# Order of the attention products within a step of a fused feed-forward and attention stage

## The reference

```python
x = x + 0.5 * ffn(layernorm(x))
x = x + attn(layernorm(x))
x = x + 0.5 * ffn(layernorm(x))

def attn(z):                                  # windows of 64 rows, 16 heads of 16
    q, k, v = split(z @ w_qkv)
    q, k = rmsnorm(q) * ln_w, rmsnorm(k) * ln_w
    att = softmax(causal(q @ k.T / 4))
    return (att @ v) @ w_proj

def ffn(z):                                   # 8 experts, 2 a row, capacity 640, and a shared part
    shared = (silu(z @ sg) * (z @ su)) @ sd   # 2048 hidden columns
    return shared + routed(z, router, rg, ru, rd)   # 1024 hidden columns an expert
```

## Time and profile before

| | us |
|---|---|
| median of 3 runs | 2125.52 (2121.11 to 2128.36) |
| profiled execution | 2136.3 |
| its span in the trace | 2134.6 |
| TensorE matmul busy | 2091.1 (98%) |
| VectorE busy | 1356.4 (64%) |
| ScalarE busy | 963.4 (45%) |
| GpSimd busy | 491.3 (23%) |

### The profile page before, as it was taken

How to read it: one execution, slowest core, us unless ns; L and a number is a source line. 1 busy time by engine, 2 the same in 40 slices (tenths; PEclk the granted TensorE clock), 3 DMA queues, 4 the chain that set the end, 5 groups by cost and what they waited for, 6 DMA issues and landing times.

```text
span 2134.6 us, 37638 instructions
## 1 busy us (share of the span) xinstructions
PE 2091.1 (98%) x13844; PEld 1910.7 (90%) x13844; DVE 1356.4 (64%) x3108; ACT 963.4 (45%) x1910; POOL 491.3 (23%) x433
## 2 busy tenths in 40 slices
PE   8999999999999999999998999999999999999999
PEld 7888899999998788888887887888999999988888
DVE  7666556666665688887888876666466666633333
ACT  3333235555553566556665542333455555522222
POOL 2423211121212232233334433222112211200000
PEclk9999999999999999999999999999999999999999
DMA  9231225554446344443544432231245444441010
GB/s 272 96 120 58 75 63 131 133 144 108 104 94 186 93 105 109 114 119 91 121 111 124 114 107 78 71 98 39 78 104 114 102 96 110 118 124 60 30 60 20
DMA packets 295976, 218.70 MB, mean 102 GB/s; under 512 B 69241, under 2 KB 276525, under 8 KB 295792
## 3 DMA queue, kind: packets, MB, share of 16 engines
q1 hardware_dynamic: 278128, 194.92, 32.5%
q0 software_dynamic: 17664, 21.38, 5.8%
HBM read 129.48 MB, written 93.23 MB: 104 GB/s over the span
## 4 chain that ended last, share of the span: by engine, by line
PE 86%; DVE 7%; issue 3%; POOL 2%; DMA 1%; SPq 1%; ACT 0%; another core or an unknown queue 0%; DVEq 0%; POOLq 0%; ACTq 0%
PE gate_up_p L347 28%; PE quad L347 25%; PE out_p L385 22%; PE misc L385 4%; PE quad L555 2%; PE quad L570 1%; PE misc L539 1%; PE misc L411 1%; PE quad L571 1%; DVE qk L1154 1%; DVE p_s L1169 1%; DVE h_s L1034 1%; PE misc L422 1%; POOL w L1406 1%; PE misc L403 1%
## 5 line engine op out<-in xcount | busy, mean ns | idle before, releaser
L347 PE MATMUL gate_up_p<-zh,w 128*128 128x512 f32 (+2 forms) x2368 | 705.5, 360 | 3.2 <-DVE h_s L1034 2.4
L721 ACT CAST hh<-h_s 128x512 fp32r<-128x512 f32 (+2 forms) x511 | 276.1, 540 | 699.6 <-DVE h_s L1034 631.3
L347 PE MATMUL quad<-zh,w 128*128 128x512 f32 (+2 forms) x1728 | 481.9, 346 | 0.0
L347 PEld LDWEIGHTS gate_up_p<-zh,w 128*128 128x128 f32 x2368 | 431.2, 189 | 53.8 <-DVE h_s L1034 3.7
L385 PE MATMUL out_p<-w,hh 128*128 128x256 f32 x2808 | 458.3, 282 | 5.9 <-DVE hl L1050 3.1
L385 PEld LDWEIGHTS out_p<-w,hh 128*128 128x128 f32 x2808 | 402.9, 189 | 29.3 <-DVE hl L1050 5.7
L347 PE MATMUL gate_up_p<-zl,w 128*128 128x512 f32 (+2 forms) x1184 | 422.8, 357 | 0.0
L1050 DVE TENSOR_TENSOR hl<-h_s,hh 128x512 fp32r<-128x512 f32 (+2 forms) x431 | 247.2, 573 | 136.5 <-ACT hh L721 120.3
L1034 DVE TENSOR_TENSOR h_s<-gate_up_p,sg_s 128x512 f32<-128x512 f32 (+2 forms) x296 | 178.5, 603 | 241.4 <-PE gate_up_p L347 223.6
L347 PEld LDWEIGHTS quad<-zh,w 128*128 128x128 f32 x1728 | 308.6, 188 | 24.8
L347 PE MATMUL quad<-zl,w 128*128 128x512 f32 (+2 forms) x864 | 295.5, 342 | 0.0
(11 more groups left out here) (189 smaller groups left out, 2530.5 us busy)
## 6 DMA issues: line engine op xcount, KB each, us to landing
stage<-in_L_ffn_rg SPq DMA_DIRECT2D x128, 128.0 KB
stage<-in_L_ffn_ru SPq DMA_DIRECT2D x128, 128.0 KB
stage<-in_L_ffn_rd SPq DMA_DIRECT2D x128, 128.0 KB
heads_d<-qkh SPq DMA_DIRECT2D x128, 128.0 KB
q_t<-heads_d SPq DMA_DIRECT2D x32, 384.0 KB, 4.6
k_t<-heads_d SPq DMA_DIRECT2D x64, 192.0 KB, 4.8
slots_d<-empty SPq DMA_DIRECT2D x16, 662.5 KB, 7.6
zh_d<-zh SPq DMA_DIRECT2D x16, 512.0 KB
```

The source lines that it names most:

```text
L347: last = pe.matmul(dst, a, b, start=(k == 0), stop=(k == 3 * n - 1))
L721: nc.scalar.copy(hh[:, n % 2, 0:ncol], h_s[:, n % 2, 0:ncol]).then_inc(sm["hh_done"], 1)
```

## The change

Three engines' orders within a step change; the instructions stay the same.

- TensorE: the probability transposes come ahead of y's, the q and k product ahead of the projection; the v product comes after up(n); the value products come last in the step, after down(n) and the z transposes. The new waits: q and k wait for `a_ysum`, v for `a_vl` of the tile before. New order: gate(n), [early down], probability transposes, y transposes, q and k product, projection, up(n), v product, [late down], gate(n+1), head transposes, scores, up(n+1), preparation, down(n), z transposes, value products.
- ScalarE: silu(n) ahead of `yh`.
- VectorE: both parts of the preparation (`others`) come early, ahead of `yl`; `pl` ahead of the addition to x; `normal` after `values_low`; the row sums and their reciprocal after the heads' low part, just ahead of masking; `azl` ahead of `outputs`.

```diff
-            def qkv(t, out):
+            def qk_products(t, out):
                 if out is None:
                     pe.wait_ge(sm["a_zl"], t + 1)
                     wait(pe, sm["a_masked"], t - 1)
+                else:
+                    pe.wait_ge(sm["a_ysum"], out + 1)
+                split_product(quad[:, 0, :], [(azh[:, k, :], azl[:, k, :], aw[:, 0, k, 0:2 * C], aw[:, 1, k, 0:2 * C])
+                                              for k in range(KC)], KC).then_inc(sm["a_qk"], 1)
+
+            def v_product(t, out):
+                wait(pe, sm["a_vl"], t)
+                if out is not None:
+                    pe.wait_ge(sm["a_o"], out + 1)
+                split_product(quad[:, 1, 0:C], [(azh[:, k, :], azl[:, k, :], aw[:, 0, k, 2 * C:3 * C], aw[:, 1, k, 2 * C:3 * C])
+                                                for k in range(KC)], KC).then_inc(sm["a_v"], 1)
...
                 gate(n, b % 2, c, buf, SB)
-                if out is not None:
-                    y_transpose(out)
                 if early_down:
                     down_of(*chunk_before(f, phase, b, c))
                 if probs is not None:
                     prob_transposes(probs, z, uses)
                 if out is not None:
+                    y_transpose(out)
+                if z is not None:
+                    qk_products(z, out)
+                if out is not None:
                     project(out)
+                up(n, b % 2, c, buf, SB)
                 if z is not None:
-                    qkv(z, out)
-                up(n, b % 2, c, buf, SB)
+                    v_product(z, out)
...
-                if probs is not None:
-                    values(probs, z, keys, out)
                 if c == 0:
                     out_free(f, phase, b)
                 down_of(f, phase, b, c)
...
                     z_transpose(ahead, uses_by(pf, pb, c + 1))
+                if probs is not None:
+                    values(probs, z, keys, out)
...
+                silu(n, SB)
                 if out is not None:
                     act.wait_ge(sm["a_yt"], out + 1)
                     wait(act, sm["a_x"], out)
                     nc.scalar.copy(yh[:, :, :], chunks(quad[:, 1, 0:C])).then_inc(sm["a_yh"], 1)
-                silu(n, SB)
...
-                if ahead is not None and c:
-                    normal(ahead)
+                if s:
+                    others(s - 1, 0)
+                    others(s - 1, 1)
+                if ahead is not None and not c:
+                    stats(ahead)
+                if out is not None:
+                    dve.wait_ge(sm["a_yh"], out + 1)
+                    v.tensor_tensor(yl[:, :, :], chunks(quad[:, 1, 0:C]), yh[:, :, :], ALU.subtract).then_inc(sm["a_yl"], 1)
+                if probs is not None:
+                    dve.wait_ge(sm["a_ph"], probs + 1)
+                    v.tensor_tensor(pl[:, :, :], pairs, ph[:, :, :], ALU.subtract).then_inc(sm["a_pl"], 1)
                 if out is not None:
                     dve.wait_ge(sm["a_x"], out + 1)
                     v.tensor_tensor(xtile(out), quad[:, 1, C:2 * C], xtile(out), ALU.add).then_inc(sm["a_o"], 1)
...
-                if z is None or c:
-                    h_product(n, SB)
-                if z is not None and c:
+                h_product(n, SB)
+                if z is not None:
                     qk_normal(z)
+                if z is not None:
                     values_low(z)
...
+                if ahead is not None:
+                    normal(ahead)
                 if c:
                     fused_low(n)
                 if z is not None:
                     heads_low(z)
+                if probs is not None:
+                    row_sums(probs)
+                    inverse_sums(probs)
                 if keys is not None:
                     masked(keys)
...
                 banks(s)
-                if probs is not None:
-                    outputs(probs)
                 if ahead is not None:
                     dve.wait_ge(sm["a_zh"], ahead + 1)
                     v.tensor_tensor(azl[:, :, :], chunks(misc[:, 1, 0:C]), azh[:, :, :], ALU.subtract).then_inc(sm["a_zl"], 1)
+                if probs is not None:
+                    outputs(probs)
                 fused_low(n + 1)
```

More of the change, by code:

```diff
@@ L546, in scores @@
                     pe.wait_ge(sm["a_vl"], z + 1)
-                elif out is not None:
+                if out is not None and z is None:
                     pe.wait_ge(sm["a_o"], out + 1)
@@ L1212, in fused_step @@
                 n = chunk(f, phase, b, c)
-                if out is not None:
-                    dve.wait_ge(sm["a_yh"], out + 1)
-                    v.tensor_tensor(yl[:, :, :], chunks(quad[:, 1, 0:C]), yh[:, :, :], ALU.subtract).then_inc(sm["a_yl"], 1)
                 if ahead is not None and c:
@@ L1231, in fused_step @@
                     v.tensor_tensor(xtile(out), quad[:, 1, C:2 * C], xtile(out), ALU.add).then_inc(sm["a_o"], 1)
[L1232 to L1235, removed]
-                if probs is not None:
-                    row_sums(probs)
-                    inverse_sums(probs)
-                    dve.wait_ge(sm["a_ph"], probs + 1)
-                    v.tensor_tensor(pl[:, :, :], pairs, ph[:, :, :], ALU.subtract).then_inc(sm["a_pl"], 1)
-                if ahead is not None and not c:
-                    normal(ahead)
                 if z is not None:
@@ L1246, in fused_step @@
                     v.tensor_scalar(qke[:, :], ssq[:, :], 1.0 / C, RMS_EPS, ALU.mult, ALU.add).then_inc(sm["a_qke"], 1)
-                if z is None or c:
-                    h_product(n, SB)
-                if z is not None and c:
+                h_product(n, SB)
+                if z is not None:
                     qk_normal(z)
+                if z is not None:
                     values_low(z)
-                elif z is not None:
-                    values_low(z, (0,))
-                    qk_normal(z)
-                    values_low(z, (1,))
-                    h_product(n, SB)
-                others(s - 1, 1)
+                if ahead is not None:
+                    normal(ahead)
                 if c:
```

## The result

| | before | after |
|---|---|---|
| median, us (same chip) | 2126.6 | 2192.7 (2188.8 to 2193.8) |
| ratio to before, 95% interval | | 1.0317 [1.0301, 1.0333] |
| span of the profiled execution | 2134.6 | 2187.1 |
| the profiled execution itself | 2136.3 | 2188.8 |

The change costs 66 us. The forecast was 2168, and the time lies above its range (2131 to 2186). Its sign and its mechanism hold. Two terms of its sum don't: the one for the clock, which was nothing, and the one for the preparation, which was +4.

A forecast was written before the change was run, and what follows sets the result against it. TensorE was taken to bound regular work in the fused stage. Regular blocks +37, preparation +4 and tail +3 made +44 us on the profiled execution; against the median 2125.5, less a little, 2168 us, range 2131 to 2186.

The forecast's parts named there:

- p to M: Regular step, from projection start (p) to masking start (M): M = p + 8.2 us, with row sums and reciprocal now before masking.
- M to the exponential, M to y: After masking start: exponential ends M + 5.6 us, `half_s` runs M + 5.63 to 6.9, multiply by 1/sum due M + 5.8.
- The blocked end: VectorE held by GpSimd's `half_s`: multiply ends M + 7.2, low part M + 8.35, against 6.2 and 6.85 us without blocking.
- c = 0 pairs: Steps c=6 to c=0 to c=2: 37.5 us with blocking, 35.4 without, 34.0 before; TensorE waits of 2.8, 0.7 and 0.6 us.
- Clock: Falls to the 1.2 GHz level after TensorE waits: some 1.7 us each, none in the sum, up to five in the range.
- Preparation: Next feed-forward's preparation, from step 26: some 20 us exposed ahead of `yl`, less waits that go; +4, between -8 and +10.
- A: The forecast case: blocking and late value products, 2168 us, 2150 to 2186 by preparation's bounds and clock falls; chance 0.58.
- Silu's table load on y's path: ScalarE, silu ahead of `yh`: table load 1.28 us on y's path, binding only without blocking, projection then at M + 8.3.
- Rival D: Silu's table load costs more than its 1.28 us; an end wait at each switch would give 2208 us; chance 0.03.
- B: The multiply by 1/sum gets ahead of `half_s` (margin 0.2 us): +13, 2138 us; chance 0.22.
- C: Faster: VectorE slack absorbs preparation, `x` and values waits go; -14 and +6 from regular steps, 2118 us; chance 0.08.
- E: The orders don't matter, new waits only take over from those removed: 2122 to 2130 us; chance 0.09.

The follow-up runs named there:

- root first: Changed kernel with GpSimd making the layer norm's root for the tile ahead before the probabilities' row halves: 2164.0 us, ratio 1.0179.
- Early down behind q,k: Changed kernel with the c = 0 early down product behind the q,k product, its two VectorE instructions behind the addition to x: 2176.0 us, ratio 1.0246.
- The filled wait: Changed kernel with six extra 512-column products, result unread, ahead of the early down product at c = 0: 2185.2 us, ratio 1.0293.

## Why the prediction was right and wrong

- **p to M, M to the exponential, M to y: right.** Multiply due M + 5.8, low part M + 8.35 and projection M + 9.5 were drawn; 5.8, 8.25 and 9.5 came, and even steps of 17.8 us against 17.7.
- **The blocked end was the right one to take.** The multiply takes 1.14 us in the mean of the regular steps, and root first moves it back to 0.43 with 27.3 us of steps 8 to 28. The row at 959.30 shows a wait until 0.29 us after `half_s` ends. The rule cited from the Trainium skill, "SBUF — State Buffer" (section "SBUF: two separate sides"), agrees with the trace.
- **c = 0 pairs: 37.5 forecast, 38.0 without a clock fall, 39.3 with one.** The waits of 2.8, 0.7 and 0.6 came as 2.64, 0.65 and 0.56. Early down behind q,k showed that the first of them is not additive: removed, it gives 0.9 us a block.
- **The missing 25 us, by stretch.** The forecast's +44 was taken to the median, less a little. Against the repeated profile of the kernel before (2118.1) the change is 69.0 us in span: 3.9 ahead of step 8, 37.0 in steps 8 to 28 (forecast 26.5, five blocks), 28.5 in 28 to 39 (17.6: two blocks, 4 and 3), -0.4 behind. The 3.9 come from the measuring point: gate(n) of step 8 itself starts 2.6 us earlier than before. Of the 10.5 too many in steps 8 to 28, 6.9 lie in the four regular blocks (28.1 against 21.2: three clock falls, and 0.75 a block in step sizes) and 3.6 in the fifth, which holds a fall and the first preparation. Against the first profile it looks like 52.5, which would have hidden 16 of the 25.
- **Clock: the step "none taken in the sum" failed.** The term was put at nothing although the forecast itself named waits of 2.8 us in eight steps. Two low-clock stretches became 12 (the first profile had four): four more in steps 8 to 28 and six more in 28 to 39. The filled wait shows what three of them cost, 3.9 us. At that 1.3 us, or the 1.7 of the forecast, the ten are 13 to 17 us (estimate). The range took five.
- **Preparation: "+4, between -8 and +10" failed too.** Moving it back gives 13.3 us in steps 24 to 39 and 16.9 between medians, with about as many low-clock stretches (13 against 12). The forecast set a cost of some 20 us against a credit of some 15 for waits that would go. The waits for `x` did go, but from 1108 to 1360 us TensorE waits 22.0 us for `yl` and 15.4 for `hl`, where the largest wait before was the 5.0 for `x`; on balance the credit wasn't there. The two terms together cover the missing 25 us, and may overlap in steps 28 to 39; how they share it there isn't separated.
- **The upper bound.** From its own terms, 2168 + 6 for the preparation + 5 x 1.7 for the clock, A's range ends at 2182.5, so the 2186 had little to spare.
- **Silu's table load on y's path: right that it isn't bound there, but its worth was missed.** Only `yh` was followed. The load holds `ph`, `pl` and `x` as well, 26 us. Rival D's drain didn't show: silu starts 0.02 us after its load here, and 0.01 in the earlier trace rows. The Trainium skill, "ScalarE: Activation LUTs" (What ACT_TABLE_LOAD costs), has such a drain; no run here shows it.
- **Rivals.** B is refuted by the multiply's 1.14 us, and its price for the regular part was right (16.4 and 35.9 in the root-first run against 16.5 and 35.4). C is refuted by the time; its own sign, VectorE idle ahead of `yl`, doesn't come either (at 1158.98 `yl` follows L865 at once). E is refuted by the ratio.

## What to carry to other kernels

When a VectorE instruction with its operands in SBUF is moved later, look at what GpSimd runs at the new time, and at who waits for the instruction there; 0.2 us of margin decided some 27 us here. When waits vanish from a list, ask which instruction behind them is next late, and count them as moved until a run shows otherwise. Give falls of the clock a price in the sum where the change brings new waits of TensorE: four of six waits of 2.6 us had one here, at 1.3 us each. Profile the kernel before twice where a difference of 10 us matters.

## What the hardware showed beyond expectation

- An instruction of two elements a partition is held as a large one is. In the root-first run the scale of the sums (L1249) takes 0.65 us beside `quarter_s`, 0.16 elsewhere, while `pl`, with one operand in PSUM, runs at its usual length (1.23 us) beside `half_s`. GpSimd, then VectorE:

```profile
965.77 1.30 POOL L1412 TENSOR_TENSOR half_s<-p_s 128x512 f32<-128x512 f32 x1
967.15 0.75 POOL L1415 TENSOR_TENSOR quarter_s<-half_s 128x256 f32<-128x256 f32 x1
```
```profile
965.80 1.23 DVE L1242 TENSOR_TENSOR pl<-misc,ph 128x1024 fp32r<-128x1024 f32 x1 [0.17 <-ACT ph L794]
...
967.27 0.65 DVE L1249 TENSOR_SCALAR qke<-ssq 128x2 f32<-128x2 f32 x1
```

- TensorE's clock fell to 0.50 behind four of the six waits of 2.6 us at c = 0 in steps 8 to 28, and behind none of them when six wide products stood in the same place and left 1.3 us of the wait.
